# First attention of a four-layer model: tile pipeline of five cycles instead of nine, slots by a table's eight maxima, statistics of x in pairs

## The reference

```
x = x + _L0_xattn_ref(_layernorm(x, axis=-1), ctx_1024, ctx_1024, mask_BxSxS2_bk1, ...)   # 16 heads, 77 context rows
x = x + _L0_ffn_ref(_layernorm(x, axis=-1), L0_ffn_router_w, ...)

E, K, F = (64, 8, 192)
C = 128
logits = x.astype(jnp.float32) @ router_w.T
probs = jax.nn.softmax(logits, axis=-1)
topk_w, topk_ids = jax.lax.top_k(probs, K)
topk_w = topk_w / jnp.sum(topk_w, axis=-1, keepdims=True)
...
pos = jnp.cumsum(onehot, axis=0)[jnp.arange(N), flat_e] - 1
valid = pos < C
idx = jnp.where(valid, flat_e * C + pos, E * C)
x_buf = jnp.zeros((E * C + 1, x.shape[1]), x.dtype).at[idx].set(x[tok])
...
shared = jax.nn.silu(sg) * su @ ws_down
return routed + shared
```

## Time and profile before

| | us |
|---|---|
| median of 3 runs | 2310.17 (2302.4 to 2310.84) |
| profiled execution, its time | 2307.27 |
| its span | 2305.5 |
| mean granted TensorE clock | 0.941 |
| first attention, start to the first expert transpose | 282.77 |

### The profile page before, as it was taken

The page is one execution under the profiler, slowest core; times in us unless marked ns, Lnnn a source line. Parts: engine busy times, 40 slices in busy tenths (PEclk is TensorE's granted clock), DMA queues, the critical chain, the costliest instruction groups (busy, mean ns, idle before and its releaser), DMA issues. The chain is left out here.

```text
span 2305.5 us, 39301 instructions
## 1 busy us (share of the span) xinstructions
PE 2068.5 (90%) x12908; PEld 1542.6 (67%) x12908; DVE 1118.2 (49%) x4098; ACT 927.2 (40%) x2962; POOL 629.7 (27%) x568
## 2 busy tenths in 40 slices
PE   7996899786899989899989979879997899599998
PEld 4764487554566645466655558768886577499997
DVE  4886244355777732477754358722221465411111
ACT  3652132233677731277753135422221466233332
POOL 0377556522222210122210002222223022212222
PEclk9997799878999999999999979979998899699999
DMA  6701299875740020100000081111121800376662
GB/s 221 282 18 34 88 322 341 230 256 181 280 174 11 10 63 0 39 8 11 12 12 1 1 312 50 42 42 27 33 39 14 289 29 34 116 217 182 182 180 51
DMA packets 161357, 255.34 MB, mean 111 GB/s; under 512 B 36937, under 2 KB 123956, under 8 KB 160246
## 3 DMA queue, kind: packets, MB, share of 16 engines
q1 hardware_dynamic: 131734, 224.62, 28.2%
q0 software_dynamic: 29424, 28.21, 7.0%
HBM read 165.95 MB, written 101.04 MB: 116 GB/s over the span
## 5 line engine op out<-in xcount | busy, mean ns | idle before, releaser
L2685 ACT ACTIVATE m3e_ht<-m3e_h_bank,m3w_b 128x128 f32<-128x128 f32 x312 | 89.2, 368 | 190.0 <-PE m3e_h_bank L2657 190.0
L3290 ACT ACTIVATE la_probs<-la_probs,la_nb,la_invnorm 128x256 f32<-128x256 f32 x256 | 150.2, 594 | 0.2 <-DVE la_nb L3206 0.2
L2668 PE MATMUL m3e_y_bank<-m3w_w,m3e_ht 128*128 x624 | 141.0, 379 | 0.0
L906 POOL DMA_INDIRECT m_xbuf<-m0w_rows,m0w_slots x128 | 127.4, 995 | 37.5 <-issue 35.7
L2839 ACT ACTIVATE m2e_ht<-m2e_h_bank,m2w_b 128x270 f32<-128x270 f32 x128 | 62.3, 487 | 179.8 <-PE m2e_h_bank L2804 179.8
L2632 POOL DMA_INDIRECT out<-m3e_y,m3e_dest x39 | 60.3, 1547 | 240.0 <-DVE m3e_y L2720 232.0
L2668 PEld LDWEIGHTS m3e_y_bank<-m3w_w,m3e_ht 128*128 128x128 f32 x624 | 115.7, 190 | 14.1
L2779 POOL DMA_INDIRECT m_sum<-m2e_y,m2e_dest x48 | 70.2, 1463 | 200.3 <-DVE m2e_y L2887 194.9
L2697 DVE COPY m3e_xt<-m3e_turned_bank 128x256 f32<-128x256 f32 x39 | 16.6, 425 | 220.8 <-PE m3e_turned_bank L2645 220.8
L2804 PE MATMUL m2e_h_bank<-m2e_xt,m2w_w 128*128 128x270 f32 x512 | 122.4, 397 | 0.0
L2460 POOL DMA_INDIRECT m_sum<-m0e_y,m0e_dest x64 | 98.9, 1545 | 83.2 <-DVE m0e_y L2569 52.2
(11 more groups left out here) (499 smaller groups left out, 4836.3 us busy)
## 6 DMA issues: line engine op xcount, KB each, us to landing
m3w_w<-in_m_w SPq DMA_DIRECT2D x32, 1024.0 KB, 6.8
m0w_wgu<-in_m_gu SPq DMA_DIRECT2D x32, 768.0 KB, 10.0
m_xbuf<-all_zeros SPq DMA_DIRECT2D x38, 528.0 KB, 6.1
m2w_w<-in_m_w SPq DMA_DIRECT2D x16, 1024.0 KB, 12.2
m3e_w<-in_m_w SPq DMA_DIRECT2D x15, 1024.0 KB, 6.1
m0e_wd<-in_m_down SPq DMA_DIRECT2D x32, 384.0 KB, 11.1
m_xbuf<-all_zeros SPq DMA_DIRECT2D x16, 576.0 KB, 6.4
m0w_xb<-m_xbuf SPq DMA_DIRECT2D x32, 288.0 KB, 7.9
```

The source lines that it names most:

```text
L906: nc.gpsimd.indirect_dma_start(k.slot_buffers[m.name][0][:, :], bass.IndirectOffsetOnAxis(ahead.slots[:, t, i:i + 1], 0), ahead.rows[t % R ...
L2668: last = nc.tensor.matmul(y_ps[t % 2][0:R, 0:D], h_t[t % 2][:, c, :], ahead.w2[:, bass.ts(e, 1), c, :].rearrange("p o f -> p (o f)"), star ...
L2685: last = nc.scalar.activation(h_t[t % 2][:, 4 * half + i, :], h_ps[t % 2][half][:, i * R:(i + 1) * R], m.act, bias=ahead.b1[:, bass.ds(e * ...
L3290: last = nc.scalar.activation(probs[u][:, hh, :], probs[u][:, hh, :], ACT.Exp, bias=nb[u][:, hh:hh + 1], scale=inv_norm[u][:, hh:hh + 1], ...
```

## The change

The order of work in the first attention is written anew as cycles c = -1 to T + 1. In cycle c TensorE runs turn_p(c), turn(c+2), count(c-2), two score groups of c+1, value(c), return_x(c-1), the third score group of c+1, turn_o(c), route_x(c-1), project(c). A tile is turned in cycle c-2, valued and projected in c, returned and ranked in c+1, placed and scattered in c+2. ScalarE's exponentials are split around recopy and copy_o. VectorE's list starts a cycle with the statistics behind the addition and the placing of tile c-2.

The chosen flags now come from `match_replace` (the eight largest logits are overwritten in a copy) and a not-equal with the logits. The slots come from a table of 64 columns: (100000 - 128*expert - position), times room (position below 128) and chosen; its eight maxima, taken from 100000, are the eight slots. The statistics of x are taken in pairs of tiles: pair 1 in cycle -1, pairs 2 and 3 in cycle 0, 4 to 6 in cycle 1, 7 in cycle 2, with one root on POOL for a pair. SyncE issues wv, bv, bo and wo ahead of its wait for the split context, half of the zeroing ahead of the split bias and half behind it, and the shared weights behind both. The shared gate/up parts are spread between the last counts; the two `hide` come behind the loop.

```diff
+STAT_PAIRS = {0: (2, 3), 1: (4, 5, 6), 2: (7,)}
...
+                sp.dma_start(wv[:, :, :], d["wv"]).then_inc(wo_in, 16)
+                sp.dma_start(bv[:, :], d["bv"]).then_inc(wo_in, 16)
+                sp.dma_start(bo[:, :], d["bo"]).then_inc(wo_in, 16)
+                sp.dma_start(wo[:, :, :], d["wo"]).then_inc(wo_in, 16)
                 sp.wait_ge(split, 5)
...
+                xbuf, zeroed, pieces, _ = k.slot_buffers[m.name]
+
+                def zero_slots(i):
+                    sp.dma_start(xbuf[i * 4 * P:(i + 1) * 4 * P, :].rearrange("(p a) d -> p (a d)", p=P), k.zeros[:, 0:4 * PAYLOAD]).then_inc(zeroed, 16)
+
+                for i in range(pieces // 2):
+                    zero_slots(i)
                 sp.wait_ge(split, 10)
                 for i in range(3):
                     sp.dma_start(bo_dram[i:i + 1], bpart[i][:, :]).then_inc(bo_out, 16)
                 sp.wait_ge(bo_out, 48)
                 sp.dma_start(bo3[:, :], bo_dram).then_inc(bo_in, 16)
-                zero_slot_buffers(k, sp, ("m0",))
+                for i in range(pieces // 2, pieces):
+                    zero_slots(i)
+                sp.dma_start(wgu[:, :, :], md["sgu"].rearrange("(c p) f -> p c f", p=P)).then_inc(shared_in, 16)
+                sp.dma_start(wd[:, :], md["sd"][0:P]).then_inc(shared_in, 16)
+                sp.dma_start(wd_rest[:, :], md["sd"][P:F]).then_inc(shared_in, 16)
                 for i, total in enumerate(ahead.sums):
                     for c in range(0 if i else SUM_ROWS // 512 - 1, SUM_ROWS // 512):
                         sp.dma_start(total[c * 512:(c + 1) * 512, :].rearrange("(p a) d -> p (a d)", p=P), k.zeros[:, 0:4 * D]).then_inc(ahead.sum_zeroed, 16)
...
+                def power_x(p):
+                    pool.wait_ge(x_stat, 6 * (p + 1))
+                    nc.gpsimd.tensor_tensor(k.rstd[:, 2 * p:2 * p + 2], k.var[:, 2 * p:2 * p + 2], k.minus_half[:, 0:2], ALU.pow).then_inc(x_powered, 1)
...
-                for step in range(T + 9):
-                    if step + 2 < T:
-                        power_x(step + 2)
-                    if 0 <= step - 4 < T:
-                        power(step - 4)
-                    if 0 <= step - 8 < T:
-                        scatter(step - 8)
+                for c in range(1, T + 2):
+                    for p in STAT_PAIRS.get(c - 1, ()):
+                        power_x(p)
+                    if c - 1 < T:
+                        power(c - 1)
+                    if c >= 2:
+                        scatter(c - 2)
...
-                def rank_onehot(t):
-                    dve.wait_ge(ranked, 5 * t + 3)
-                    nc.vector.tensor_tensor(onehot[t % 3][:, :, :], k.iota[:, 0:E].unsqueeze(1).broadcast_to([P, K, E]),
-                                            idxf[t % 3][:, :].unsqueeze(2).broadcast_to([P, K, E]), ALU.is_equal).then_inc(ranked, 1)
...
+                def rank_left(t):
+                    dve.wait_ge(ranked, 3 * t + 1)
+                    nc.vector.match_replace(left[:, :], ahead.top[:, t, :], ahead.logits[:, t, :], -3.0e38).then_inc(ranked, 1)
...
-                    nc.vector.tensor_reduce(chosen[t % 2][:, :], onehot[t % 3][:, :, :].rearrange("p k e -> p e k"), AX, ALU.max).then_inc(ranked, 1)
+                    nc.vector.tensor_tensor(chosen[t % 2][:, :], left[:, :], ahead.logits[:, t, :], ALU.not_equal).then_inc(ranked, 1)
...
-                def pick(t):
+                def place_room(t):
                     dve.wait_ge(counted, t + 1)
-                    dve.wait_ge(scored, NG * (min(t + 6, T - 1) + 1))
-                    nc.vector.tensor_tensor(picked[:, :, :], onehot[t % 3][:, :, :], pos_ps.unsqueeze(1).broadcast_to([P, K, E]), ALU.mult).then_inc(picking, 1)
+                    nc.vector.scalar_tensor_tensor(room[:, :], pos_ps, float(m.cap), chosen[t % 2][:, :], ALU.is_lt, ALU.mult).then_inc(picking, 1)
+                    if t == 0:
+                        dve.wait_ge(ends_made, 1)
+                    nc.vector.tensor_tensor(slot_of[:, :], ends[:, :], pos_ps, ALU.subtract).then_inc(picking, 1)
 
...
-                    nc.vector.tensor_reduce(ahead.pos[:, t, :], picked[:, :, :], AX, ALU.add).then_inc(picking, 1)
+                    dve.wait_ge(picking, 4 * t + 2)
+                    nc.vector.tensor_tensor(slot_of[:, :], slot_of[:, :], room[:, :], ALU.mult).then_inc(picking, 1)
...
+                    nc.vector.max(last8[:, :], slot_of[:, :]).then_inc(picking, 1)
...
+                    nc.vector.tensor_scalar(ahead.slots[:, t, :], last8[:, :], -1.0, NOWHERE, ALU.mult, ALU.add).then_inc(placed, 1)
...
+                stats_pair(0)
+                norm(0)
+                norm(1)
+                for c in range(-1, T + 2):
+                    at(c - 1, add)
+                    at(c - 2, rank_sum)
+                    at(c - 1, add_stats)
+                    at(c - 2, rank_index)
+                    at(c - 1, add_aggr)
+                    at(c - 2, rank_float)
+                    at(c - 1, add_eps)
+                    at(c - 2, place_room)
+                    at(c - 2, carry_names)
+                    at(c - 2, place_pos)
+                    at(c - 2, carry_total)
+                    at(c - 2, place_slot)
+                    at(c - 2, carry_weights)
+                    at(c - 2, place)
+                    at(c + 1, mask, 0)
+                    at(c + 1, maximum, 0)
+                    at(c + 1, mask, 1)
+                    at(c - 1, renorm)
+                    at(c + 1, maximum, 1)
+                    if c == -1:
+                        mask(0, 2)
+                        maximum(0, 2)
+                        split_bo()
+                        stats_pair(1)
+                    at(c + 3, norm)
+                    for p in STAT_PAIRS.get(c, ()):
+                        stats_pair(p)
+                    at(c, invert)
+                    at(c, unload)
+                    if c >= 0:
+                        at(c + 1, mask, 2)
+                        at(c + 1, maximum, 2)
+                    at(c - 1, log)
+                    at(c - 1, rank_top)
+                    at(c - 1, rank_left)
+                    at(c - 1, rank_shift)
+                    at(c - 1, rank_chosen)
...
+                copy_x(0)
+                for c in range(-1, T + 2):
+                    at(c, copy_p)
+                    at(c + 2, copy_x)
+                    if c <= T:
+                        at(c - 2, soften)
+                    at(c + 1, exp, 0, 0, 6)
+                    at(c + 1, exp, 1, 6, 9)
+                    at(c - 1, recopy)
+                    at(c + 1, exp, 1, 9, 12)
+                    at(c, copy_o)
+                    at(c + 1, exp, 2, 12, 16)
+                gate_shared(0)
+                soften(T - 1)
...
+                turn(0)
+                for c in range(-1, T):
+                    at(c, turn_p)
+                    at(c + 2, turn)
+                    at(c - 2, count)
+                    at(c + 1, score, 0)
+                    at(c + 1, score, 1)
+                    if c == -1:
+                        score(0, 2)
                         outputs()
-                    if step == T + 3:
-                        pe.wait_ge(shared_in, 48)
-                        pe.wait_ge(exped, NG * T)
-                        pe.wait_ge(p_copied, 3 * T)
-                        shared_gate_up(0)
-                    if step == T + 6:
-                        pe.wait_ge(added, T)
-                        pe.wait_ge(logged, T)
-                        shared_gate_up(1)
+                    at(c, value)
+                    at(c - 1, return_x)
+                    if c >= 0:
+                        at(c + 1, score, 2)
+                    at(c, turn_o)
+                    at(c - 1, route_x)
+                    at(c, project)
+                pe.wait_ge(shared_in, 48)
+                pe.wait_ge(exped, NG * T)
+                pe.wait_ge(p_copied, 3 * T)
+                shared_part(0, 0)
+                count(T - 2)
+                shared_part(0, 1)
+                shared_part(0, 2)
+                return_x(T - 1)
+                route_x(T - 1)
+                shared_part(1, 0)
+                count(T - 1)
+                pe.wait_ge(added, T)
+                shared_part(1, 1)
+                pe.wait_ge(logged, T)
+                shared_part(1, 2)
```

More of the change, by code:

```diff
@@ L970, in norm @@
                 def norm(t):
-                    dve.wait_ge(x_powered, t + 1)
+                    dve.wait_ge(x_powered, t // 2 + 1)
                     if t >= 2:
@@ L1391, in shared_gate_up @@
                     for j in range(3):
[L1392 to L1395 removed]
+                        shared_part(c, j)
                 def shared_down(c):
```

201 lines of the change are left out of this document (63 added, 138 removed).

## The result

The changed kernel takes 2289.76 us (median of 6 runs, 2280.97 to 2292.24) beside 2304.45 us (2302.4 to 2310.84) of the kernel before in the same series: ratio 0.9927, 95% interval 0.9911 to 0.9944, 14.7 us or 0.7% less. In the profiled execution (2289.92 us, span 2288.1) the first expert transpose starts at 268.06 instead of 282.77, 14.7 us earlier. The first expert stage behind it is as long as before (170.2 and 170.4 us from its first transpose to its last indirect add), the last scores of the local attention come 15.1 us earlier, and the next two expert stages start 17.5 and 17.3 us earlier. So the first stage carries the gain. The other 2.7 us of the difference between these two executions (spans 2305.5 and 2288.1) arise in stages that the change doesn't touch.

The account below looks back on a forecast made before the run. POOL's scatters and roots, 10.88 us a tile, were taken to hold the first attention. Shared down 18.7 earlier, minus 1.0 for clock, plus 2.7 at the end: 20.4 us less, so 2288 us (forecast 2279 to 2294; range 2277 to 2304).

Parts of the forecast that it names:

- wo early: Kernel start: wait for wo and slow clock go; first transposes at 32.5 us (bounds 32.5 to 35), 9.7 us won.
- Cycles 0 to 2: First cycles: 13.2 and 13.4 us with statistics waits, cycle 2 from 59.1, first scatter at 63.0 against 98.27.
- wrong if past 70: Sign at the first scatter: expected near 63 us, forecast wrong if it comes past 70.
- start gated: Rival: zeros, bias or a fallen clock in cycles 0 and 1 put first scatter at 73, total 2297; chance 0.10.
- clock arm: Part of the start rival: clock falls in the gaps of cycles 0 and 1, delaying first scatter; no separate chance.
- covers for zeros and bias: Before first scatter: zeroing done at 55 us, bias back at 43 for project at 44.5; covers of 8 and 1.5.
- VectorE's operations: Slot arithmetic per tile: 3.3 us out, 1.5 in; DVE from about 9.0 to 7.3 us, earning nothing by itself.
- slower: Rival: DVE's in-order waits put scores and exponentials in series, 13.3 us a cycle, total 2321; chance 0.08.
- The steady cycle: Middle of the stage: TensorE's natural cycle 10.3 to 10.6 us; POOL's 10.87 holds from about cycle 6.
- The tail: Stage end: shared down from 223.3 us, TensorE done at 260.4, first expert transpose at 262.4 against 282.77.
- Given back: Rival: the expert stage is bound by the DMA engines and absorbs the early start, total 2308; chance 0.05.
- port: Rival: each tile's norm and renorm stop POOL in full, 14 us on 16 tiles, total 2302; chance 0.03.

Follow-up runs that it names:

- roots: Changed kernel with GpSimd's second roots (tile 2 on) placed inside the scatter stream instead of behind all scatters of the tiles before; ratio 0.9919 to the kernel before.
- onehot: Changed kernel with the old slot arithmetic (one-hot table of 8x64 columns) in the new order of tiles; ratio 1.0097 to the kernel before.
- tail: Changed kernel with the shared expert's gate and up of columns 2 and 3 ahead of the first down product; ratio 0.9911 to the kernel before.
- new_again: The changed kernel unchanged, run again in a later series; ratio 0.9938 to the kernel before.
- delay: Changed kernel with ten unused root operations on GpSimd ahead of the first scatter; first expert transpose at 278.92 us, one execution.
- half: Changed kernel with GpSimd issuing four of each tile's eight scatters; first expert transpose at 256.42 us, one execution.
- wo_late: Changed kernel with the transfers of wv, bv, bo and wo back behind the split wait and its loads; ratio 0.9961 to the kernel before.
- stats: Changed kernel with the x statistics of tile pairs 1 to 7 moved from the block to where VectorE is idle; ratio 0.9901 to the kernel before.
- both5: Changed kernel with the edits of roots and stats together, each root two scatters earlier; ratio 0.9845 to the kernel before.
- table: Kernel before with only the new slot arithmetic (64-column table, value replacement, eight maxima); ratio 0.9995 to the kernel before.
- new: The changed kernel itself in its first series; 2289.76 us, ratio 0.9927 to the kernel before.
- both: Changed kernel with the edits of roots and stats together; ratio 0.9851 to the kernel before.

## Why the prediction was right, point by point

The time came out at 2289.8 for 2288, inside the forecast's own range, and by its own chances the change was to be faster with 0.72. That it came so near is in part luck. The forecast was 22.2 us under the 2310.17 that was known of the kernel before; with three more runs that kernel's median is 2304.45, and the gain is 14.7. The stage moved 14.7 us where the sum said 20.4. What was right is the mechanism: a stage ended by GpSimd's stream of scatters and roots, begun earlier, with TensorE's dense tail as the new end. Its steps:

- *wo early.* Half right. The gap is gone, but the scores and the outputs then ran partly at half clock, and the first transposes start at 35.21, at the poor end of my 32.5 to 35. In *roots*, *onehot*, *tail* and *new_again*, with the same start, it was 32.4 to 33.2, in *delay* and *half* 34.6 and 35.6: the value that I took was the good end of what this start does. Having wo early is worth 3 us of stage in the profiles and 5 us of median (*wo_late*).
- *Cycles 0 to 2.* This is the step that missed in size: 15.7 and 14.6 us for 13.2 and 13.4. Both waits of my sum, 1.8 for x and 2.7 for the statistics, belong to cycle 0, and cycle 1 was priced by the same count. In cycle 0 the first measured 1.40, and the second isn't there: TensorE ran at half clock from 37.92 to 46.40, and VectorE's four tiles of statistics were done when the values were (where less of that cycle was slow, in *roots* and *wo_late*, the second wait was 1.7 us). In cycle 1, with six tiles' statistics in a block, the wait was 3.17. So what the sum lacked is the clock: I had priced the work of both cycles at full clock. With the start at 35.2 instead of 32.5 this puts cycle 2 at 65.5 instead of 59.1. The first scatter came 5.2 us into the cycle, not 3.9. The counts were made 3.1 us in and not 1.8, as that cycle began at half clock too (2.34 us for ten transposes); VectorE then took 1.1 us for my 2.1; and 1.0 us passed between the slots and the start of the scatter, which I hadn't counted. In *stats*, at full clock, it was 5.0 us too, as VectorE took statistics ahead of the slots there. Sum: 70.67 for 63.0. My own line "wrong if past 70" was crossed, and the rival "start gated" (first scatter at 73) is nearer to this profile than the forecast is. Its clock arm holds. Its covers for zeros and bias held here: GpSimd waited for the slots and for nothing else, and project of cycle 0 waited only 0.51 us, for no transfer. How thin the cover for the bias is, *both5* shows. Its project of cycle 0 was ready 1.55 us before 43.25 and waited for the bias until then, which is when I had it back (43):

```profile
43.25 0.39 PE L1393 MATMUL a_pt_bank<-a_bo,all_ones 3*128 3x256 bf16 x1 [1.55 <-DMA a_bo<-a_dram_bo]
```

- *VectorE's operations.* The size was right: 3.3 out and 1.5 in made 1.8, and *table* shows 9.75 less 7.99 = 1.76. In the new kernel the seven, with the load of the eight values (0.09), take 0.09+0.21+0.22+0.22+0.21+0.22+0.21+0.35 = 1.7 us. But VectorE is busy 8.1 us a tile in the new order (*half*) and not 7.3; that surplus of 0.8 us isn't longer operations. Summed one by one, a tile's records make 9.9 us in *half* and 9.7 in *table* without the three of x's statistics. What differs is by how much neighbouring records overlap: 1.7 us a tile in *half*, 2.5 in *table*. In the new order the copy of the logits, their eight maxima and the replacement, each in need of the one before, stand side by side, and each starts 0.03 to 0.04 us after the one before has ended (130.14, 130.39 and 130.65 us in *half*); in *table* others stand between them, and neighbours overlap by up to 0.1 us. "It pays for the extra waits of the shorter pipeline" was true in a stronger sense than I meant: without it the loop has the price of the "slower" rival (13.3 us a cycle and 2321 predicted for that, 13.7 and 2327.7 measured for *onehot*). The way there is another: not scores and exponentials in series, but the residual add behind the one-hot, and the clock.
- *The steady cycle.* TensorE's natural cycle is 10.0 (its own work 9.87), not 10.3 to 10.6; the hole of 0.4 us between turn_o and project isn't there. GpSimd's 10.87 holds from cycle 5 (said: 6). The last root came 152.15 us behind the first scatter, within 0.03 of 14*10.87. *half* and *roots* confirm the reason.
- *The tail.* From the last root to shared down I had 8.1 us (215.2 to 223.3): measured 222.82 to 230.90, 8.1. The allowance of 1.0 us for the clock wasn't needed, and from 230.90 to the end of TensorE's work it is 35.6 us for 36.0. The last gap measured 1.56 for 2.0. So 7.7 us of miss at the start, 2.0 won back here: 5.7 of the 20.4.
- *Given back, port.* Neither shows. The expert stage is as long as before (170.4 us for 170.2). The scatter takes 974 ns at the median (976 in the earlier trace rows) with VectorE busy 61 of 80 us, and the stream of 128 is 172.2 us long (173.2 before). The Trainium skill (SBUF — State Buffer, § Who interferes with whom) has VectorE's copies and tensor_scalars, where they run in a two-port mode, lock GpSimd out of the port of its descriptors; a price of that beyond the 10.87 us a tile doesn't show in any run here, and no run tells in which mode these operations run.
- The stage won 14.7 us for a first scatter 27.6 earlier: the missing 12.9 are the tail. Before, the stage ended 11.3 us behind the last scatter; now TensorE's dense part ends it, 25.2 behind. The sum had that in it (GpSimd's end at 236.9, TensorE's at 260.4; measured 243.8 and 266.5), and *roots* takes it away again.

## What to carry to other kernels

When one engine's queue is the pace, look at what stands in it and not only at how full it is: here a 0.6 us root that others wait for stood behind eight scatters that nobody waits for, and moving it forward gave 9 us without shortening the queue. Work that is moved out of the loop goes into gaps that the trace of the changed order shows, one small piece to each; in one block ahead of a value that TensorE waits for, it costs the wait and then the fallen clock (4.6 us of waits here, and 11.2 us of start when they were gone). And test a bundle by its corners: here neither half of the change was worth anything without the other.

## What the hardware showed

- In all eight profiles with the block of statistics, the TensorE gap of 3.2 us in cycle 1 is followed by ten transposes at 1.2 GHz (2.34 us for 1.31). A cycle without any gap can still run wholly at 0.50 (18.28 us in *new_again*), while the same cycle took 11.7 us in *new*. In *onehot*, of three cycles that follow each other, the first two have the same gap of 1.4 us and the third has none; their clock was 1.00, 0.60 and 0.88. In *stats*, with gaps of at most 0.89 us in the first cycles, it stayed at 1.00 from 30 to 200 us; with the same gaps *both* shows 0.83 from 40 to 50.
- Value replacement over 64 columns takes 0.21 us and its load of eight values 0.09; eight maxima over 64 columns 0.21 us, as long as an ordinary 64-column operation. A maximum over the 8x64 one-hot takes 1.02 us.
- The indirect scatter of 128 rows keeps GpSimd 0.97 us and 0.30 us of issue in every stretch of these kernels; a root is 0.6 us long between two tiles' scatters and up to 0.95 us among them (*both5*); the stream is 2 to 3 us longer with the roots among them in all (*roots* 175.5, *both* 174.8, *both5* 175.4, for 172.2).
